# Attention of a small vision transformer: transposed keys, near scores on TensorE, and another order of the halves

## What is computed

```python
h = patches_with_shifts(x)                 # shifted patch tokens, LayerNorm, projection to 192
n = layernorm(h)
q, k, v = split(n @ qkv_w.T + qkv_b)       # 12 heads of 16
a = softmax(where(mask, q @ k.T * 16 ** -0.5, -inf))
h = h + (a @ v) @ out_w.T + out_b
n2 = layernorm(h)
h = h + sum over the 2 best of 8 experts of gate * (gelu(n2 @ w1 + b1) @ w2 + b2)
```

## Time and profile before

| | us |
|---|---|
| median of 3 runs | 205.86 |
| lowest and highest | 205.37, 206.51 |
| the profiled execution, its own time | 205.97 |
| its span, first to last instruction | 204.3 |
| mean granted clock of TensorE | 0.933 |
| TensorE busy | 182.2 |
| VectorE busy | 147.1 |
| ScalarE busy | 116.2 |
| POOL busy | 78.2 |

### The profile page before, as it was taken

One profiled execution on the slowest core, in us unless ns is written; L12 is line 12 of the kernel. 1 busy time (PEld: TensorE's weight loads), 2 busy tenths in 40 slices (PEclk: granted clock), 3 DMA queues, 4 the chain that ended last, 5 costly groups with the idle time before them and its releaser, 6 DMA issues.

```text
span 204.3 us, 3431 instructions
## 1 busy us (share of the span) xinstructions
PE 182.2 (89%) x1136; PEld 161.7 (79%) x1136; DVE 147.1 (72%) x327; ACT 116.2 (57%) x204; POOL 78.2 (38%) x90
## 2 busy tenths in 40 slices
PE   0799996965999777589999999999999999999994
PEld 0798495955987547368898999998989999989894
DVE  4299896397358985857747886976878859868753
ACT  2297736024464331259568759679677596795540
POOL 7782002441500669512006533536265335362000
PEclk9997899795899967679999999999999999999999
DMA  6999998000000960044000071170440710000002
GB/s 132 224 353 296 242 245 161 0 0 0 2 3 0 279 145 0 5 134 136 0 3 0 0 226 44 48 221 2 142 128 0 225 45 2 0 3 0 0 0 79
DMA packets 14059, 17.99 MB, mean 88 GB/s; under 512 B 2311, under 2 KB 10112, under 8 KB 14046
## 3 DMA queue, kind: packets, MB, share of 16 engines
q1 hardware_dynamic: 13502, 17.80, 32.7%
q10 hardware_dynamic: 544, 0.03, 0.2%
HBM read 17.44 MB, written 0.39 MB: 87 GB/s over the span
## 4 chain that ended last, share of the span: by engine, by line
PE 66%; DVE 12%; SPq 8%; DMA 5%; issue 3%; POOL 3%; ACT 1%; DVEq 0%; POOLq 0%
PE ps L364 33%; PE ps L1080 16%; PE ps L1082 7%; DMA stage<-in_L_ffn_w 5%; SPq L395 2%; DVE norm L1315 2%; PE ps L919 2%; PE ps L808 1%; PE ps L1125 1%; PE ps L1124 1%; PE ps L1123 1%; DVE shifted L1160 1%; POOL rs L511 1%; SPq L350 1%; DVE sc L1156 1%
## 5 line engine op out<-in xcount | busy, mean ns | idle before, releaser
L364 PE MATMUL ps<-big_r,wsplit 128*128 128x512 f32 (+1 forms) x250 | 63.8, 392 | 0.0
L1080 PE MATMUL ps<-wsplit,big_r 128*128 128x384 f32 x168 | 49.5, 354 | 0.0
L364 PEld LDWEIGHTS ps<-big_r,wsplit 128*128 128x128 f32 x250 | 43.9, 194 | 6.6
L1156 DVE TENSOR_TENSOR big_r<-early,big_r 128x512 fp32r<-128x512 f32 x48 | 36.0, 752 | 18.3 <-ACT big_r L326 17.7
L724 ACT ACTIVATE early<-ps,b1t 128x512 f32<-128x512 f32 x48 | 32.8, 682 | 27.6 <-PE ps L364 27.6
L1082 PE MATMUL ps<-wsplit,big_r 128*128 128x192 f32 x168 | 42.1, 251 | 0.0
L1082 PEld LDWEIGHTS ps<-wsplit,big_r 128*128 128x128 f32 x168 | 32.0, 190 | 1.4
L1080 PEld LDWEIGHTS ps<-wsplit,big_r 128*128 128x128 f32 x168 | 31.5, 188 | 1.5
L326 ACT ACTIVATE big_r<-early 128x512 fp32r<-128x512 f32 x48 | 30.5, 635 | 1.5
L1489 DVE SCALAR_TENSOR_TENSOR merge<-sq,gates,merge 128x192 f32<-128x192 f32 x32 | 26.9, 864 | 0.0
L308 POOL TENSOR_TENSOR wsplit<-stage,wsplit 128x768 fp32r<-128x768 f32 x4 | 7.4, 1845 | 36.1 <-ACT wsplit L326 18.9
(11 more groups left out here) (222 smaller groups left out, 310.3 us busy)
## 6 DMA issues: line engine op xcount, KB each, us to landing
stage<-in_L_ffn_w SPq DMA_DIRECT2D x4, 576.0 KB, 6.4
early<-in_L_ffn_w SPq DMA_DIRECT2D x4, 576.0 KB, 5.6
shifted<-in_L_tok_w SPq DMA_DIRECT2D x6, 288.0 KB, 8.7
early<-in_x SPq DMA_DIRECT2D x3, 512.0 KB, 6.6
stage<-in_L_ffn_w SPq DMA_DIRECT2D x4, 384.0 KB, 4.1
stage<-in_L_ffn_w SPq DMA_DIRECT2D x8, 192.0 KB, 5.0
early<-in_L_ffn_w SPq DMA_DIRECT2D x4, 384.0 KB, 3.2
early<-in_L_ffn_w SPq DMA_DIRECT2D x8, 192.0 KB, 4.3
```

Of the source, the lines that this page charges most:

```text
L364: mm = nc.tensor.matmul(dst, lhs, rhs, start=(n == 0), stop=(n == 4))
L1080: nc.tensor.matmul(ps[:, AB[t], 0:2 * D], g_hi[:, j % NG, tok], w2c, start=(f == 0), stop=False)
L1156: return nc.vector.tensor_tensor(o, a, b, op)
```

## The change

- **Near scores.** `token_major`'s q and k, the biased q and k, `previous_k_v` and the VectorE reductions go. Keys are made transposed for all tokens of a half (`transposed_k`). VectorE multiplies them by the transposed queries, once in place and once shifted by one column (`near_products`, four instructions of 128 or 64 rows by 256 columns for each half). TensorE sums each product over a head's rows with a 0/1 matrix, into four column tiles of 32 (`near_by_heads`); ScalarE copies the result, and a product with another 0/1 matrix (`place`) adds it to the scores' bank (`near_scores`).
- **Masks.** ScalarE lays the mask out, and a product with the identity writes it to each half's bank first (`masks`); strided and near scores are added to it in PSUM. `scores` keeps the maximum and the subtraction. Scores and exponentials are stored head by head.
- **Values.** Made for each tile; the strided ones are selected from them (`sel`). The values of the previous token come by two SBUF-to-SBUF DMAs per tile from SP. `v_s`, `key_rep` and `previous_k_v` go.
- **Order.** VectorE, ScalarE, POOL and TensorE take the halves in turn. POOL waits for each half's own tiles; its w2 split of expert 0 waits for the first half's low parts alone; its splits of expert 1 move behind the second norm's last low parts. ScalarE's copies for expert 0 move ahead, three of expert 1's and the Gelu table load move to between the attention's high parts and the second norm's.
- **Constants.** The row goes into the projection's bank by a product (`constant_rows`), and POOL's addition (line 547) goes.
- **Idle products.** Three times three products of 128 x 512, whose result nobody reads, around the transposes and the projection of the second half (`keep_busy`).
- `EARLY` is 3 instead of 2, and `layer1(0, 2)` behind the router's transposes goes. PSUM banks are dealt out anew.

```diff
     load_expert(sp, 1, 1)
     sp.wait_ge(s_sps, G)
     sp.dma_start(b2_rows, b2.rearrange("e d -> (e d)").unsqueeze(0).broadcast_to([P, E * D])).then_inc(d_b2, 16)
+    sp.wait_ge(s_first_cols, 2)
+    for t in range(TT):
+        sp.wait_ge(s_vtok, t + 1)
+        for a, z in pieces(1, P):
+            sp.dma_start(vv[a:z, t, 1], vv[a - 1:z - 1, t, 0]).then_inc(d_prev[t], 16)
     with sp.Fori(1, E // 2) as i:
...
         if g == 0:
             rstd(0, 0)
     rstd(0, 1)
-    pool.wait_ge(s_nlo, G)
+    pool.wait_ge(s_nlo, 1)
     split_low_w2(pool, 0, 0)
     def near_values(g):
...
-    near_values(0)
-    near_values(1)
+    for g in range(G):
+        pool.wait_ge(s_vtok, 2 * g + 2)
+        for t in (2 * g, 2 * g + 1):
+            pool.wait_ge(d_prev[t], 16 * len(pieces(1, P)))
+        near_values(g)
     pool.wait_ge(s_nv, G)
-    pool.wait_ge(s_row, 1)
-    pool.wait_ge(s_h, TT)
-    pool.wait_ge(s_watps, 4)
-    nc.gpsimd.tensor_tensor(hb[:], h[:], const_row[:, :].unsqueeze(1).broadcast_to([P, TT, D]),
-                            ALU.add).then_inc(s_hb, 1)
-    split_low_w1(pool, 1, 1)
     rstd(1, 0)
     rstd(1, 1)
-    split_low_w2(pool, 1, 1)
+    pool.wait_ge(s_n2lo, G)
+    split_low(pool, 1, 1)
...
+    split_high(0, 2)
     act.wait_ge(s_emb, 1)
     copy(u_part[:], ps[:, UB, 0:D]).then_inc(s_u, 1)
+    split_high(0, 3)
+    act.wait_ge(s_mask, 2)
+    copy(mask_x[:], mask[:, :].unsqueeze(1).unsqueeze(1).broadcast_to([P, 2, HEADS, NS])).then_inc(s_maskx, 1)
...
     last_columns_again(0, 0, n1)
     high_parts(0, s_nt, NTB, nt, s_nhi)
-    split_high(0, 2)
-    split_high(0, 3)
-    last_columns_again(0, 1, n1)
     act.wait_ge(d_bqk, 16 * BQK_DMAS)
     transposed_q(0)
+    last_columns_again(0, 1, n1)
+    values(0)
     high_parts(1, s_nt, NTB, nt, s_nhi)
-    token_major(0)
-    act.wait_ge(s_kst, 1)
-    nc.scalar.activation(kts[:, 0], ps[:, KB, 0:S], ACT.Identity, bias=bqk[:, 2:3]).then_inc(s_ktsb, 1)
-    nc.scalar.activation(kts[0:REM, 1], ps[0:REM, KB, S:2 * S], ACT.Identity,
-                         bias=bqk[0:REM, 3:4]).then_inc(s_ktsb, 1)
-    copy(v_s[:], ps[0:S, KB, 2 * S:2 * S + D]).then_inc(s_vssb, 1)
-    token_major(1)
+    near_rows(0)
     transposed_q(1)
-    previous(0)
+    exponentials(0)
+    near_rows(1)
+    transposed_p(0)
+    values(1)
+    exponentials(1)
+    transposed_p(1)
     act.wait_ge(s_emb, G + 1)
     act.wait_ge(d_stage[1], 16 * STAGE_DMAS)
     split_high(1, 0)
-    split_high(1, 1)
-    token_major(2)
-    previous(1)
-    token_major(3)
-    previous(2)
-    split_high(1, 2)
-    split_high(1, 3)
-    previous(3)
-    exponentials(0)
-    transposed_p(0)
-    exponentials(1)
-    transposed_p(1)
     for g in range(G):
         act.wait_ge(s_ao, g + 1)
         copy(ao[:, 2 * g:2 * g + 2, D:], ao[:, 2 * g:2 * g + 2, P:D]).then_inc(s_aodup, 1)
         high_parts(g, s_at, ATB, aot, s_ahi)
+    nc.scalar.activation(table_in[:], neg_half[:, 0:1], ACT.Gelu)
+    split_high(1, 1)
+    split_high(1, 2)
+    split_high(1, 3)
     for g in range(G):
         last_columns_again(1, g, n2)
         high_parts(g, s_n2t, N2B, n2t, s_n2hi)
-    nc.scalar.activation(table_in[:], neg_half[:, 0:1], ACT.Gelu)
     def pair(i, last, first=False):
...
+    def near_by_heads(g):
+        pe.wait_ge(s_qtsb, 2 * g + 2)
+        pe.wait_ge(s_prod, 4 * g + 4)
+        for n, m in enumerate((P, REM)):
+            for s in range(2):
+                q = 2 * n + s
+                mm = nc.tensor.matmul(ps[32 * q:32 * q + 32, NB[g], 0:TG], head_of_row[0:m, :],
+                                      qk_prod[0:m, g, s, n], start=True, stop=True)
+        mm.then_inc(s_nearps, 1)
...
+    def keep_busy(count):
+        for _ in range(count):
+            nc.tensor.matmul(ps[:, N2B[1], :], wat[:, 0, 0:P], wat[:, 0, 0:512], start=True, stop=True)
...
+    def constant_rows(g):
+        pe.wait_ge(s_pt, g + 1)
+        nc.tensor.matmul(ps[:, OB[g], 0:2 * D], ones_f[0:1, :],
+                         const_row[0:1, :].unsqueeze(1).broadcast_to([1, 2, D]), start=True, stop=False)
...
-    previous_k_v(0)
-    pe.wait_ge(s_vssb, 1)
-    strided_scores(0)
-    token_major(2)
-    previous_k_v(1)
-    token_major(3)
-    previous_k_v(2)
-    repeated_v(0)
-    repeated_v(1)
-    strided_scores(1)
-    previous_k_v(3)
-    repeated_v(2)
-    repeated_v(3)
...
+    pe.wait_ge(s_u, 1)
+    pe.wait_ge(s_urow, 1)
+    pe.wait_ge(s_meansq, 1)
+    masks(0)
+    masks(1)
+    transposes(0, n1, s_n, lambda t: t + 1, NTB, s_nt, s_ndup)
+    pe.wait_ge(s_watlo, 4)
+    pe.wait_ge(s_wathi, 5)
+    pe.wait_ge(d_bqk, 16 * BQK_DMAS)
+    for n, (col, part) in enumerate(((0, 0), (0, 1), (1, 2))):
+        mm = nc.tensor.matmul(ps[:, VBB, 0:D], bias_v[:, col:col + 1].broadcast_to([P, P]),
+                              wat[:, part, OUT0:OUT0 + D].bitcast(F32), start=(n == 0), stop=(n == 2))
+    mm.then_inc(s_vbias, 1)
+    pe.wait_ge(s_t2, 2)
+    pe.wait_ge(s_nhi, 1)
+    pe.wait_ge(s_nlo, 1)
+    transposed_q(0)
+    transposed_k(0)
+    values(0)
+    values(1)
+    pe.wait_ge(s_row, 1)
+    transposes(1, n1, s_n, lambda t: t + 1, NTB, s_nt, s_ndup)
+    strided_scores(0)
+    near_by_heads(0)
+    pe.wait_ge(s_t2, TT)
+    pe.wait_ge(s_nhi, 2)
+    pe.wait_ge(s_nlo, 2)
+    transposed_q(1)
+    near_scores(0)
+    transposed_k(1)
+    repeated_v(0)
+    repeated_v(1)
+    strided_scores(1)
+    near_by_heads(1)
+    transposed_p(0)
+    values(2)
+    values(3)
+    near_scores(1)
+    strided_values(0)
+    repeated_v(2)
+    repeated_v(3)
+    constant_rows(0)
+    transposed_p(1)
+    transposes(0, ao, s_ao, lambda t: t // 2 + 1, ATB, s_at, s_aodup)
+    strided_values(1)
+    constant_rows(1)
+    projection(0)
+    pe.wait_ge(s_vbd, TT)
+    keep_busy(3)
+    transposes(1, ao, s_ao, lambda t: t // 2 + 1, ATB, s_at, s_aodup)
+    keep_busy(3)
+    projection(1)
+    keep_busy(3)
...
         tt(dst[:, 1:4:2, cols], ps[:, banks[g], :].rearrange("p (k t) -> p k t", k=2),
            dst[:, 0:4:2, cols].bitcast(F32), ALU.subtract).then_inc(done, 1)
+    def key_blocks(g):
+        dve.wait_ge(d_bqk, 16 * BQK_DMAS)
+        dve.wait_ge(s_kt, g + 1)
+        for kbd, m, n, gs_ in ((kbd_a, P, 0, 8), (kbd_b, REM, 1, 4)):
+            keys = ps[0:m, KB[g], n * TG:(n + 1) * TG:STRIDE]
+            nc.vector.scalar_tensor_tensor(
+                out=kbd[0:m, g], in0=keys.unsqueeze(1).broadcast_to([m, gs_, 4 * NK]),
+                scalar=bqk[0:m, 2 + n:3 + n],
+                in1=head_of_row[0:m, 0:gs_].unsqueeze(2).broadcast_to([m, gs_, 4 * NK]),
+                op0=ALU.add, op1=ALU.mult).then_inc(s_kbd, 1)
     patch_statistics(0)
     dve.wait_ge(s_urow, 1)
...
     less_mean(1)
+    low_parts(0, s_nhi, NTB, nt, s_nlo)
     embedding(1)
-    low_parts(0, s_nhi, NTB, nt, s_nlo)
     statistics(0, 1, h, s_h, lambda t: t + 1)
+    dve.wait_ge(d_rows, 16)
+    dve.wait_ge(s_vbias, 1)
+    tt(const_row[:], ps[:, VBB, 0:D], outb_row[:], ALU.add).then_inc(s_row, 1)
+    key_blocks(0)
     normalised(0, 1, h, n1)
-    dve.wait_ge(d_rows, 16 * 2)
-    low_parts(1, s_nhi, NTB, nt, s_nlo)
-    def biased_q_k(t):
...
+    def near_products(g):
+        dve.wait_ge(s_first_cols, 2)
+        dve.wait_ge(s_qtsb, 2 * g + 2)
+        for n, m in enumerate((P, REM)):
+            for s in range(2):
+                nc.vector.scalar_tensor_tensor(
+                    out=qk_prod[0:m, g, s, n, s:TG], in0=ps[0:m, KB[g], n * TG:(n + 1) * TG - s],
+                    scalar=bqk[0:m, 2 + n:3 + n], in1=qt[0:m, n, g * TG + s:(g + 1) * TG],
+                    op0=ALU.add, op1=ALU.mult).then_inc(s_prod, 1)
...
-    biased_q_k(0)
-    key_blocks()
-    biased_q_k(1)
-    near_scores(0)
-    biased_q_k(2)
-    near_scores(1)
-    biased_q_k(3)
+    near_products(0)
+    low_parts(1, s_nhi, NTB, nt, s_nlo)
     scores(0)
-    near_scores(2)
+    key_blocks(1)
+    near_products(1)
     v_blocks(0)
     v_blocks(1)
-    near_scores(3)
+    denominators(0)
     scores(1)
+    outputs(0)
     v_blocks(2)
     v_blocks(3)
-    denominators(0)
-    outputs(0)
     denominators(1)
+    low_parts(0, s_ahi, ATB, aot, s_alo)
     outputs(1)
-    dve.wait_ge(s_vbias, 1)
-    tt(const_row[:], ps[:, ATB[1], 0:D], outb_row[:], ALU.add).then_inc(s_row, 1)
-    low_parts(0, s_ahi, ATB, aot, s_alo)
-    low_parts(1, s_ahi, ATB, aot, s_alo)
     def residual(g):
-        dve.wait_ge(s_hb, 1)
         dve.wait_ge(s_op, g + 1)
         ts = slice(2 * g, 2 * g + 2)
-        tt(h2[:, ts], hb[:, ts], ps[:, OB[g], 0:2 * D].rearrange("p (t n) -> p t n", t=2),
+        tt(h2[:, ts], h[:, ts], ps[:, OB[g], 0:2 * D].rearrange("p (t n) -> p t n", t=2),
            ALU.add).then_inc(s_h2, 1)
         statistics(1, g, h2, s_h2, lambda t: t // 2 + 1)
     residual(0)
+    low_parts(1, s_ahi, ATB, aot, s_alo)
     normalised(1, 0, h2, n2)
     residual(1)
     low_parts(0, s_n2hi, N2B, n2t, s_n2lo)
```

269 lines of the change are left out of this document (109 added, 160 removed).

## The result

The changed kernel took 213.4 us (median of 4 runs, 210.3 to 217.2) where the kernel before took 205.6 beside it: a ratio of 1.029 [1.022, 1.036]. Measured once more with the last group of experiments, it was 211.9 against 204.9, 1.025 [1.018, 1.032]. I had forecast 208.4 with a range to 211.2: the sign was right, the size was not, and both medians lie above the range. The ratios leave disturbed runs out; since the granted clock is part of what differs here, I also compare medians over all runs, each with that of the kernel before beside it: 1.038 and 1.034 for the changed kernel, in the mean 1.036. The profiled execution took 214.9, with a span of 213.2.

A forecast was written before the change was run, and what follows sets the result against it. TensorE's expert products bound the kernel, so the change pays by when the first starts. Terms -0.3 + 2.6 + 1.0 - 1.7 + 0.9 = +2.5 on 205.97 gave 208.5, or 208.4 beside the median; range 203.6 to 211.2.

The forecast's parts named there:

- To the scores: Up to TensorE's scores of the second half: done at 65.3 us, -0.3 us, bounds 62 and 66.5.
- the term for the clock: Before the second half's scores: 64.0 us at full clock, 65.6 if TensorE's clock falls in the wait.
- POOL's split: First norm: POOL's w2 low split holds up the second half's norm, ready at 53.4 us instead of 50.5.
- To POOL's last sum: From the second half's scores to POOL's last sum of near values: 11.1 us instead of 8.5, +2.6.
- the last output: From POOL's last near sum to VectorE's last attention output: 2.2 us instead of 1.25, +1.0.
- the bias rows landing first: SP's queue after the scores: shifted rows land behind the 768 KB of bias rows, first two tiles 5.1 us after the scores.
- To the last low parts: From the last attention output to the second norm's last low parts: 13.4 us instead of 15.1, -1.7.
- ScalarE's block: Before the second norm's copies: table load and three weight copies, 3.6 us together; first half's columns wait 2 us.
- my 11.9 and 14.5: Last output to last low parts: 11.9 us with the clock up; 14.5 with ScalarE's copies and a slower clock return.
- To the first expert product: From the last low parts: 5.4 us instead of 4.5, +0.9; 0.1 or 2.6 depending on POOL's third piece.
- The expert loop, held unchanged: Everything behind the first expert product: 109.3 us of TensorE work, not changed by the diff.
- the third rival: Before the first expert product: POOL's third piece gets in, TensorE waits 3 us; 210.1, near 212 with another clock fall; chance 0.18.

## Why the prediction was wrong

**To the scores (forecast 65.3, profiled 65.75): right, with the term for the clock too small.** POOL's split held the norm as I said (1.88 us; I had argued from a norm of 2.97). At full clock I had 64.0 from a norm at 44.25, 19.8 us, and 20.1 was measured. For the fall I had added 1.6 us; it was 3.0. It was hidden by luck: the stage began 1.6 us earlier than before. TensorE was at half clock for 3.4 us of the embedding instead of 7.1, and that differs by execution: with the same embedding code the first norm starts anywhere from 42.2 to 44.8 us in the kernels above.

**To POOL's last sum (forecast 11.1 us behind the scores, measured 10.9) and the last output (2.2, measured 2.0): right, for a wrong reason in one part.** That SP's wait makes the first half wait for the second was the step, and undoing it gives back 4.6 us. But I put the rows' start down to the bias rows landing first; it is four issues at SP and 2 us of landing. Had I moved the bias rows alone, I would have hoped for 2 us at the last sum and got 0.5.

**To the last low parts (forecast 13.4, measured 15.3 and 14.3): failed.** I wrote that TensorE would be at half clock in the projection, which held, and that ScalarE's block makes the first half's columns wait 2 us, which held (85.55 to 87.56). I then took 13.4, between my 11.9 and 14.5, where both costs at once belonged: that term was mis-sized by 0.9 us, and once more by the second fall, at 90.3, behind TensorE's wait of 1.5 us there.

**To the first expert product (forecast 5.4, measured 7.4): failed.** I had 0.1 or 2.6 us more than before and took 0.9; measured were 0.5 without the stall and 2.9 with it. The step that failed is when the subtraction comes due: 4.2 us after the last low parts (98.15), not 3.7, and 4.1 to 4.4 in the other executions. POOL's second piece ended 3.85 after, as I had said, so its third, started at 97.95, was under way, and the subtraction stood until it was done. I had the two within 0.1 us of each other and should not have taken a value near the cheap end.

**The expert loop, held unchanged: failed.** The diff leaves it alone, but the wait in front of it took its clock: 2.6 us. I had this as the upper end of the third rival, near 212, and had left that end out of the range; it is what happened in both profiled executions of the changed kernel. That it is the clock and not the code, the loop of 109.1 us in the kernel with 20 idle products shows, which has the same wait and no fall.

So of the 8.9 us in the spans my 2.5 held POOL's first split, SP and one fall. The 6.4 that I missed are two kinds. The larger is the clock: 1.4 us more for the fall before the scores, 1.0 for the second one behind the norm, 2.6 for the one in the loop. The other is work: 2.0 at the first expert product and 0.9 of ScalarE's block; the earlier start took 1.6 off, and the rest is small. The runs of the changed kernel go with this: at a mean granted clock of 0.950 it took 209.4 and 210.3 us, at 0.943 210.8 and 211.9, between 0.936 and 0.927 213.0 to 215.0, at 0.920 217.2. What decides whether the clock falls in a given wait, and for how long, stays open: with the same order of work up to there, the products over heads behind 52 us ran at half clock in five executions and at full in four, and no experiment here controlled it.

## What to carry to other kernels

A queue that serves two halves is only as independent as its latest wait: put transfers that the first half needs ahead of any wait for the second, and count SP's time for each issue, not only the bytes. Work moved off a busy engine's path can land beside instructions of another engine that it blocks: look for a stretch in which both are idle, not for the first place in program order. And price a new wait of TensorE twice, once for itself and once for the half-clock stretch that may follow it (here a little under half its length where TensorE sets the pace), even where that stretch lies in code that the change does not touch.

## What the runs showed of the hardware that I had not expected

A subtraction of 128x4 elements took 2.45 us beside POOL's split and 0.17 alone. Eight transfers from SBUF to SBUF, two for the 127 rows of each tile, cost SP 0.55 to 0.94 us each; they landed 2.0 us after issue in the median alone, and the first three 3.6, 3.4 and 2.5 us behind 768 KB. With four idle products in a wait of 1.2 us the clock stayed up through 12 us of sparse work (one execution), where it fell with 20 of them in a longer wait, ended 1.5 us before the next work. Without the nine around the projection it stayed down for some 20 us instead of 7 to 14, and the time was the same.
